# The first loads and first products of a gated cross-attention and expert kernel, put in another order

## The reference, cut to what matters

```python
h_q = (x @ w_q.T).reshape(b, lq, H, DH)
h_k = (key_value_states @ w_k.T).reshape(b, lk, H, DH)
h_v = (key_value_states @ w_v.T).reshape(b, lk, H, DH)
score = softmax(where(m, einsum('bqhd,bkhd->bhqk', h_q, h_k) + position_bias, -inf))
out = einsum('bhqk,bkhd->bqhd', score, h_v).reshape(b, lq, H * DH) @ w_out.T
...
x = x + tanh(g_xattn[0]) * xattn(layernorm(x), ctx_4096, ...)
x = x + tanh(g_ffn[0]) * ffn(layernorm(x), ...)
```

## Time and profile before

| | |
|---|---|
| median of 3 timed executions | 985.59 us (984.22 to 986.45) |
| the profiled execution's own time | 982.18 us |
| its span, from the first to the last instruction | 980.5 us |
| mean granted clock of TensorE | 0.99 |
| PE busy, PEld busy | 946.0 us (96%), 788.9 us (80%) |
| DVE, ACT, POOL busy | 644.0, 410.3, 281.5 us |
| first product on PE starts at | 8.88 us |

### The profile page before, as it was taken

The page is one execution under the profiler, slowest core; times in us unless marked ns, Lnnn a source line. Parts: engine busy times, 40 slices in busy tenths (PEclk is TensorE's granted clock), DMA queues, the critical chain, the costliest instruction groups (busy, mean ns, idle before and its releaser), DMA issues.

```text
span 980.5 us, 13965 instructions
## 1 busy us (share of the span) xinstructions
PE 946.0 (96%) x4843; PEld 788.9 (80%) x4843; DVE 644.0 (66%) x1067; ACT 410.3 (42%) x1003; POOL 281.5 (29%) x252
## 2 busy tenths in 40 slices
PE   6999999999999899997999999999999999999995
PEld 5888888888888688886889888898989887777773
DVE  6877669766665755643768778787877777843331
ACT  5336554333332342212655464554554424324442
POOL 1353334443433323002112122222221012043364
PEclk9999999999999999998999999999999999999998
DMA  7645454645557525536747637456364148565579
GB/s 258 220 174 203 168 202 157 225 176 200 198 178 235 215 98 203 209 141 254 275 151 288 222 136 263 148 203 231 114 244 177 43 161 341 197 209 177 170 184 259
DMA packets 86643, 193.75 MB, mean 198 GB/s; under 512 B 8592, under 2 KB 29328, under 8 KB 85168
## 3 DMA queue, kind: packets, MB, share of 16 engines
q1 hardware_dynamic: 79024, 177.54, 50.5%
q0 software_dynamic: 4784, 12.58, 5.5%
q10 hardware_dynamic: 2768, 2.75, 0.8%
HBM read 121.74 MB, written 71.11 MB: 197 GB/s over the span
## 4 chain that ended last, share of the span: by engine, by line
PE 91%; DVE 4%; DMA 2%; issue 1%; ACT 1%; DVEq 0%; ACTq 0%; SPq 0%
PE ps_job L800 7%; PE ps_job L802 6%; PE ps_job L801 6%; PE ps_attn L996 6%; PE ps_score L968 6%; PE ps_attn L1231 5%; PE ps_score L842 3%; PE ps_turn L982 3%; PE ps_score L843 3%; PE ps_score L844 3%; PE ps_attn L842 3%; PE ps_attn L843 3%; PE ps_attn L844 3%; PE ps_job L1240 2%; PE ps_job L842 2%; PE ps_job L843 2%
## 5 line engine op out<-in xcount | busy, mean ns | idle before, releaser
L724 POOL TENSOR_TENSOR score_bias<-mask_bias,pos_bias 128x1024 f32<-128x1024 f32 x32 | 77.6, 2426 | 300.4 <-DVE probs L1773 199.4
L1286 ACT ACTIVATE probs<-probs,neg_max 128x128 f32<-128x128 f32 x256 | 99.5, 393 | 97.3 <-DVE neg_max L1776 97.3
L683 POOL TENSOR_TENSOR w_sum<-w_raw 128x256 f32<-128x256 f32 x30 | 22.6, 755 | 179.9 <-PE ps_score L844 72.3
L996 PE MATMUL ps_attn<-pT,v_s 128*128 128x128 f32 x512 | 62.6, 276 | 1.5 <-issue 1.2
L1231 PE MATMUL ps_attn<-ew_s,xbT 128*128 x248 | 62.3, 380 | 1.0 <-ACT xbT L1276 1.0
L968 PE MATMUL ps_score<-kq_s 128*128 128x128 f32 x512 | 62.4, 275 | 0.0
L996 PEld LDWEIGHTS ps_attn<-pT,v_s 128*128 128x128 f32 x512 | 59.8, 192 | 1.9 <-issue 1.4
L1231 PEld LDWEIGHTS ps_attn<-ew_s,xbT 128*128 128x128 f32 x248 | 44.7, 191 | 20.2 <-issue 15.0
L968 PEld LDWEIGHTS ps_score<-kq_s 128*128 128x128 f32 x512 | 59.9, 192 | 0.2
L1773 DVE TENSOR_TENSOR probs<-ps_score,score_bias 128x512 f32<-128x512 f32 x64 | 43.7, 682 | 24.4 <-PE ps_score L968 21.8
L1800 DVE TENSOR_TENSOR acc<-ps_job,acc 128x512 f32<-128x512 f32 x56 | 37.9, 686 | 29.6 <-PE ps_job L802 29.6
(11 more groups left out here) (464 smaller groups left out, 2604.4 us busy)
## 6 DMA issues: line engine op xcount, KB each, us to landing
kq<-st SPq DMA_DIRECT2D x32, 1024.0 KB, 4.2
kq_s<-kq SPq DMA_DIRECT2D x64, 512.0 KB, 4.5
v_s<-v_all SPq DMA_DIRECT2D x8, 2048.0 KB, 10.6
w_raw<-wa_dram SPq DMA_DIRECT2D x31, 512.0 KB, 5.5
v_all<-st SPq DMA_DIRECT2D x24, 512.0 KB, 3.7
y_slots<-ones SPq DMA_DIRECT2D x32, 256.0 KB, 4.6
wo_raw<-wo_dram SPq DMA_DIRECT2D x8, 1024.0 KB, 7.0
ew_s<-ew_dram SPq DMA_DIRECT2D x4, 2048.0 KB, 13.2
```

The costliest lines, as they stand in the source:

```text
L724: nc.gpsimd.tensor_tensor(score_bias[:], mask_bias[:], pos_bias[:, i % 2].unsqueeze(1).broadcast_to([P, B, P]), ALU.add).then_inc(bias_rea ...
L996: last = nc.tensor.matmul(ps_attn[half][:, cols(b)], v_s[g % 2][:, BH * half + b, cols(j)], pT[:, half, cols(b)], start=True, stop=True)
L1286: last = nc.scalar.activation(probs[i % 2][:, half, b], probs[i % 2][:, half, b], ACT.Exp, bias=neg_max[:, i % 2, half, b:b + 1], accum_ou ...
```

## The change

SP's queue now begins with the weights A11 (128 KB) and half 0 of the tokens of chunk 0 (256 KB), both counted by one new semaphore, `first_in`, then half 1 of chunk 0 (256 KB, `ctx_in[0]`); the rest follows as before. The ACT queue keeps only block 3. ACT copies in this order: A11 (after a wait for `first_in` of 32), half 0 of chunk 0, block 3, half 1 of chunk 0, then chunks 1 to 3 as before. DVE: lo of A11, lo of half 0, lo of block 3, lo of half 1. PE's products for chunk 0 of step 0 are grouped by token half. `x_in` and `router_w_in` are merged into `inputs_in`, waited for at its full count of 64.

```diff
         @block.sync
         def _(sp):
-            for c in range(C):
+            sp.dma_start(w_raw[0][:, A11], wa[0, :, A11]).then_inc(first_in, 16)
+            sp.dma_start(ctx_raw[:, 0, 0:HALF], ctxT[:, 0, 0:HALF]).then_inc(first_in, 16)
+            sp.dma_start(ctx_raw[:, 0, HALF:], ctxT[:, 0, HALF:]).then_inc(ctx_in[0], 16)
+            for c in range(1, C):
...
-                sp.dma_start(acc[:, tiles], x[tiles].rearrange("t p d -> p t d")).then_inc(x_in, 16)
-            sp.dma_start(rw_raw[:], rw).then_inc(router_w_in, 16)
-            sp.dma_start(rb_s[:], rb.partition_broadcast(P)).then_inc(router_w_in, 16)
+                sp.dma_start(acc[:, tiles], x[tiles].rearrange("t p d -> p t d")).then_inc(inputs_in, 16)
+            sp.dma_start(rw_raw[:], rw).then_inc(inputs_in, 16)
+            sp.dma_start(rb_s[:], rb.partition_broadcast(P)).then_inc(inputs_in, 16)
...
+                    def terms(r, half, some):
+
+                        psum, tok = ps_a[p][2 * r + half][:], cols(half, HALF)
+                        w_h, w_l = w_hi[p][:, blocks[r], k], w_lo[p][:, blocks[r], k]
+                        if 0 in some:
+                            nc.tensor.matmul(psum, w_h, ctx_hi[:, c, tok], start=(c == 0), stop=False)
+                        if 1 in some:
+                            nc.tensor.matmul(psum, w_l, ctx_hi[:, c, tok], start=False, stop=False)
+                            last = nc.tensor.matmul(psum, w_h, ctx_lo[:, c, tok], start=False, stop=(c == C - 1))
+                            if c == C - 1:
+                                last.then_inc(first_psum, 1)
+
+                    if s == 0 and c == 0:
+
+                        for half in range(2):
+                            pe.wait_ge(ctx_hi_done, half + 1)
+                            for r in range(2):
+                                pe.wait_ge(w_hi_done, r + 1)
+                                terms(r, half, (0,))
+                            for r in range(2):
+                                pe.wait_ge(w_split, r + 1)
+                                pe.wait_ge(ctx_split, half + 1)
+                                terms(r, half, (1,))
+                        continue
...
         @block.scalar
         def _(act):
-            for k in (A11, 3):
-                act.dma_start(w_raw[0][:, k], wa[0, :, k]).then_inc(first_w_in, 16)
+            act.dma_start(w_raw[0][:, 3], wa[0, :, 3]).then_inc(first_w_in, 16)
...
-            first_w_hi(slice(A11, A11 + 1), first_w_in, 32)
-            first_w_hi(slice(3, 4), first_w_in, 32)
-            for c in range(C):
+            first_w_hi(slice(A11, A11 + 1), first_in, 32)
+            act.wait_ge(first_in, 32)
+            copy(ctx_hi[:, 0, 0:HALF], ctx_raw[:, 0, 0:HALF]).then_inc(ctx_hi_done, 1)
+            first_w_hi(slice(3, 4), first_w_in, 16)
+            act.wait_ge(ctx_in[0], 16)
+            copy(ctx_hi[:, 0, HALF:], ctx_raw[:, 0, HALF:]).then_inc(ctx_hi_done, 1)
+            for c in range(1, C):
...
             first_w_lo(slice(A11, A11 + 1), 1)
-            first_w_lo(slice(3, 4), 2)
-            for c in range(C):
+            for half in range(2):
+                tok = slice(half * HALF, (half + 1) * HALF)
+                dve.wait_ge(ctx_hi_done, half + 1)
+                V.tensor_tensor(ctx_lo[:, 0, tok], ctx_raw[:, 0, tok], ctx_hi[:, 0, tok], ALU.subtract).then_inc(ctx_split, 1)
+                if half == 0:
+                    first_w_lo(slice(3, 4), 2)
+            for c in range(1, C):
...
                 if s in (2, 3):
-                    dve.wait_ge(x_in, 32)
+                    dve.wait_ge(inputs_in, 64)
```

More of the change, by code:

```diff
@@ L382, in sem @@
             return stack.enter_context(nc.semaphore(name))
-        ctx_in = [sem(f"ctx_in{c}") for c in range(C)]
-        x_in = sem("x_in")
+        first_in, ctx_in = sem("first_in"), [sem(f"ctx_in{c}") for c in range(C)]
         small_in, wv_last_in, v_in, wo_in = map(sem, ("small_in", "wv_last_in", "v_in", "wo_in"))
@@ L391, in build @@
         pos_in = [sem("pos_in0"), sem("pos_in1")]
-        x_res_in, router_w_in, b3_in = map(sem, ("x_res_in", "router_w_in", "b3_in"))
+        x_res_in, inputs_in, b3_in = map(sem, ("x_res_in", "inputs_in", "b3_in"))
         w12_in = [sem("w12_in0"), sem("w12_in1")]
@@ L819, in project_plain @@
                     blocks = ((A11, 3), (A12, A22))[d]
-                    pe.wait_ge(ctx_hi_done, c + 1)
+                    def terms(r, half, some):
[19 more added lines that the diff above has]
+                        continue
+                    pe.wait_ge(ctx_hi_done, c + 2)
                     pe.wait_ge(w_hi_done, 2 + d if s == 0 else 3 + s)
@@ L823, in project_plain @@
                         for half in range(2):
-                            nc.tensor.matmul(ps_a[p][2 * r + half][:], w_hi[p][:, blocks[r], k],
-                                             ctx_hi[:, c, cols(half, HALF)], start=(c == 0), stop=False)
+                            terms(r, half, (0,))
                     pe.wait_ge(w_split, 2 + d if s == 0 else 3 + s)
-                    pe.wait_ge(ctx_split, c + 1)
+                    pe.wait_ge(ctx_split, c + 2)
                     for r in range(2):
                         for half in range(2):
[L830 to L835, removed]
+                            terms(r, half, (1,))
             def product(s, psum, block, right, fresh):
@@ L1609, in _ @@
             first_w_lo(slice(A11, A11 + 1), 1)
-            first_w_lo(slice(3, 4), 2)
-            for c in range(C):
+            for half in range(2):
[5 more added lines that the diff above has]
+            for c in range(1, C):
                 if c == HALF_C:
                     first_w_lo(slice(A12, A22 + 1), 3)
-                dve.wait_ge(ctx_hi_done, c + 1)
+                dve.wait_ge(ctx_hi_done, c + 2)
                 V.tensor_tensor(ctx_lo[:, c], ctx_raw[:, c], ctx_hi[:, c], ALU.subtract).then_inc(ctx_split, 1)
@@ L1721, in _ @@
                 if s == 7:
-                    dve.wait_ge(router_w_in, 32)
+                    dve.wait_ge(inputs_in, 64)
                     chain(V.tensor_copy(rw_hi[:], rw_raw[:]))
```

## The result

The changed kernel took 981.40 us (median of 9, 979.98 to 983.24) against 985.59 (median of 9, 984.22 to 989.54) for the kernel before; the ratio is 0.9966, interval 0.9955 to 0.9977. The ratio and its interval on record make that 3.35 us less (2.3 to 4.4), a gain clear of no change but small; the two medians are 4.2 apart. The median of the kernel before is the same with nine executions as with the first three. The profiled execution took 979.98 us with a span of 978.2.

The account below looks back on a forecast made before the run. PE's line of products bounds the kernel, after one long first wait. Landing at 5.3 plus hand-over 1.05 starts PE at 6.35, 2.5 us before 8.88; the median 985.59 less that gives 983.1 us, range 981.3 to 985.4.

Parts of the forecast that it names:

- What bounds the kernel, and the order of waits: Whole kernel: a line of products on PE, 91% of the chain; before 300 us the one long wait is the first.
- The lead of 2.5 us should run through to the end: After 32 us: every load is released by a product, copy or addition, so PE's 2.5 us lead stays.
- given back: Rival: DVE slips over 1.7 us or a wait after 300 us does not move with PE; 984.9, chance 0.10.
- The hand-over: Kernel start, from landing to PE's first product: one weight copy and a 512-column copy, 1.05 us, shorter by 0.7.
- The landing: Kernel start: A11 and half 0 of chunk 0 land at 5.3 us, between 4.9 and 6.8.
- early end: First transfers, counted by bytes: landing at 4.9 us, PE starting at 5.95, a gain of 2.9 us.
- take turns row by row, whatever a row's length: First transfers: a small one on one queue and a big one on the other finish in pairs.
- Three more and smaller issues of 0.4 us ahead of them do not matter, as the bytes queued ahead stay the same: Later loads: chunk 3 still lands at 10.2 us and the weights of step 1 at 11.5.
- Whether PE keeps running: Step 0 on: no gap on PE, tightest margin 0.4 us; lo of `w_sum` ends about 29.3, needed at 31.0.
- The rival of the longer slow stretch: Rival: TensorE's 1.2 GHz stretch at the start lasts twice as long, losing 1.4 us of gain; 984.5, chance 0.08.
- The slower case: Rival: PE starts early, starves and stays at 1.2 GHz through step 0; 5.7 us slower, 991.3, chance 0.04.

Follow-up runs that it names:

- the repeat: The changed kernel once more, unaltered: ratio 0.9974 (0.9964 to 0.9985) to the kernel before; its profiled execution took 983.00 us.
- halves alone: Changed kernel with A11 back at the head of the ACT queue, keeping chunk 0's halves and products in order of arrival: ratio 0.9965 (0.9951 to 0.9978).
- the weights' place alone: Kernel before with only A11 moved to the head of the SP queue, chunk 0 whole, old product order: ratio 0.9976 (0.9967 to 0.9985).
- the run with 10 idle products: Changed kernel with 10 identity-times-itself products ahead of PE's first wait: 978.41 us, ratio 0.9955 (0.9942 to 0.9969) to the kernel before.
- the best version measured here: Changed kernel with A11 back on the ACT queue and 9 idle products ahead of PE's first wait: 977.26 us, ratio 0.9944 (0.9930 to 0.9958).
- one sized too long: Kernel before with 42 idle products ahead of PE's first wait, running on to 12.40 us: ratio 1.0025 (1.0016 to 1.0035).

## Why the prediction was right, point by point

- **What bounds the kernel, and the order of waits**: right at the start. PE's first product moved, and nothing waited afterwards up to 300 us.
- **"The lead of 2.5 us should run through to the end"**: not seen in a trace. The first trace ended 2.3 us ahead, with a higher granted clock in three windows, and the repeat, with the clock of the kernel before, kept 1.8 us up to 868 us and ended 0.8 behind it. The timed executions, 3.35 and 2.6 us less, are what shows that a gain of about that size arrives on average. The rival "given back" named such waits after 300 us and priced them at 1.8 us.
- **The hand-over**: predicted 1.05 us from landing to PE's start, measured 5.87 - 4.84 = 1.03.
- **The landing**: the term that was mis-sized. Predicted 5.3, measured 4.84, a little before even the "early end" of 4.9 that counted bytes. The 0.4 us added to it for a cost beside the bytes was not there: 743 kB had moved by 4.7 us where 644 had before. PE's start was thus 5.87 and not 6.35, and the lead 3.0 and not 2.5. Of the 1.7 us between the forecast 983.1 and the measured 981.4 this is 0.5; the other 1.2 no term explains, and it is within what the medians scatter (the repeat gained 2.6). That the forecast gain of 2.5 lies so near 2.6 is in part luck. So is it that 981.4 lies inside the range, 0.1 us above its early end. That the queues "take turns row by row, whatever a row's length" is not borne out: with halves alone, A11 on ACT landed at 0.80 + 3.3 = 4.1 and half 0 on SP, with as many rows, at 4.6. The prediction's figure from the Trainium skill, DMA: Bandwidth & Descriptors, is given there for transfers issued by GpSimd ("Anatomy of one DMA — SWDGE (gpsimd) path"), and these are issued on SP and ACT; its 4.0 was 0.8 us early, and 5.0 to 5.2 after the correction was late.
- **"Three more and smaller issues of 0.4 us ahead of them do not matter, as the bytes queued ahead stay the same"**: wrong. The bytes do stay the same, and the issues are two more. But chunk 1 was issued 0.93 us later and landed 1.1 later, and the weights of step 1 were issued 0.5 later and landed 1.1 later. The later issue is not all of it: issued at 1.70 to 1.71, chunk 1 landed at 7.0 with the weights' place alone and at 7.8 with the halves alone. It cost nothing here, since chunk 1's copy ended at 9.1 and PE came to it at about 11, after slow products. With a fast PE, chunk 1's lo part is one of three short waits, 0.3 us in the run with 10 idle products.
- **Whether PE keeps running**: without a gap, as said. The lo of step 1's weights began at 13.76 in place of the predicted 12.6 (the later landing of the weights), and lo of `w_sum` ended at 28.30 + 1.21 = 29.5 (predicted 29.3), 2.3 us ahead of PE's need. `ct_lo` went faster than in the trace before and made up for it.
- **The rival of the longer slow stretch**: it came true in the trace (1.3 us of lead lost by step 1, priced at 1.4; 0.7 in the repeat). Whether it holds in the timed executions is not settled, as told above. The Trainium skill, TensorE: Matmul & The Clock Gate, Part 1, says that the clock's monitor runs free of the kernel's start. The two traces of the changed kernel (5.4 and 4.6 us) agree with it, the three of the kernel before (3.1 to 3.3) do not by themselves. The prediction took the slow stretch as equal on both sides, which no row supported.
- **The slower case**, PE starving at 1.2 GHz, did not come about: 13 slow products are 5 or 6 more than before, under half of the 13 more at which it would decide.

## What to carry to other kernels

At a kernel's start, count what must land and be copied before the first product can run, and cut that piece; here halving the first tile and ordering the products by it gave the whole lead, and the place of a small weight in the queues gave nothing on top. Each further issue ahead of a transfer makes its own issue about 0.45 us later, so check the second need as well as the first. PE's idle time at the start can be used to bring TensorE to 2.4 GHz: with idle products sized to end when the real data come, the best version measured here ran at 0.9944 (0.9930 to 0.9958) of the kernel before, partly at a higher granted clock later on, and one sized too long (1.0025) lost time. And before two traces are compared, compare their granted clock window by window: 1 to 2 us of their difference can come from stretches that the change does not touch.

## What was not expected of the hardware

An idle product of 128 columns with fp32 operands shows as two matmuls, about 0.21 us each at 1.2 GHz (20 matmuls in 4.13 us for 10 products). TensorE's low clock lasted from 3.1 to 6.0 us after PE's first product in the traces without idle products, while the column of the granted clock read 1.00. Later in the kernel, before its last 12 us, the granted clock fell in the same three windows (324 to 331, 451 to 460 and 845 to 870 us) in all three traces of the kernel before, and in one trace of the changed kernel only at the second. And the DMA rate from 7 to 8 us was 307 to 340 GB/s in the six traces with A11 at the head of the SP queue, and 426 to 432 in the five with the transfers of before.
